# Last FFN, second pass: rounded gelu values read in place by TensorE as fp16 halves, with a smaller part of them sent out and back

## What is computed

```python
def _quant_per_tensor(x):
    scale = jnp.maximum(jnp.max(jnp.abs(x)), MIN_RANGE) / QP     # QP = 127
    return (_ste_round(x / scale), scale)

def _qlinear(x2d, w, b):
    xq, sx = _quant_per_tensor(x2d)
    wq, sw = _quant_per_tensor(w)
    out = jnp.matmul(xq, wq.T) + b[None, :]
    return out * (sw * sx)

h = _qlinear(x.reshape(-1, D), w1, b1)      # 256 -> 1024
h = jax.nn.gelu(h, approximate=False)
o = _qlinear(h, w2, b2)                     # 1024 -> 256
x = x + jnp.tanh(g_ffn[1]) * o
```

## Time and profile before

| | |
|---|---|
| runs | 1312.6, 1309.03, 1311.22 us; median 1311.22 |
| profiled execution | 1308.02 us, of which the span of the instructions 1306.2 |
| busy: TensorE, VectorE, ScalarE, GpSimd | 1192.7, 1119.0, 1012.5, 840.1 us |
| mean granted clock of TensorE | 0.979 |
| moved by DMA | 172.00 MB |

### The profile page before, as it was taken

The page is one execution under the profiler, slowest core; times in us unless marked ns, Lnnn a source line. Parts: engine busy times, 40 slices in busy tenths (PEclk is TensorE's granted clock), DMA queues, the critical chain, the costliest instruction groups (busy, mean ns, idle before and its releaser), DMA issues.

```text
span 1306.2 us, 30953 instructions
## 1 busy us (share of the span) xinstructions
PE 1192.7 (91%) x11668; PEld 852.7 (65%) x11668; DVE 1119.0 (86%) x1829; ACT 1012.5 (78%) x1737; POOL 840.1 (64%) x1315
## 2 busy tenths in 40 slices
PE   4699999999999999999998999998799888399898
PEld 3367777777777777777764666666678666144476
DVE  3488989899999998988879899988569899889898
ACT  2388888888887887888867999996456655799897
POOL 3157687777878678687776888776026777797000
PEclk9999999999999999999999999998999889699999
DMA  9677778779778687667410000001565363076199
GB/s 154 119 155 141 170 172 158 143 143 182 139 173 158 129 188 129 124 129 127 92 44 1 1 2 1 2 2 63 171 163 125 101 157 95 1 312 267 58 403 377
DMA packets 127939, 172.00 MB, mean 132 GB/s; under 512 B 47650, under 2 KB 79522, under 8 KB 123426
## 3 DMA queue, kind: packets, MB, share of 16 engines
q1 hardware_dynamic: 127024, 169.24, 54.3%
q10 hardware_dynamic: 768, 0.79, 0.5%
HBM read 80.79 MB, written 37.22 MB: 90 GB/s over the span
## 4 chain that ended last, share of the span: by engine, by line
PE 45%; POOL 16%; DVE 15%; ACT 13%; issue 6%; DMA 3%; SPq 2%; ACTq 0%; DVEq 0%; POOLq 0%
PE psum L615 7%; PE psum L630 6%; PE psum L597 4%; ACT f_gelu L2230 4%; PE psum L585 3%; POOL rs L935 3%; PE psum L1084 3%; PE psum L642 3%; PE psum L660 3%; ACT f_gelu L2222 3%; PE psum L1125 2%; POOL a_fac L1929 2%; PE psum L560 2%; PE psum L1619 2%; DVE f_hid L1245 2%
## 5 line engine op out<-in xcount | busy, mean ns | idle before, releaser
L743 ACT ACTIVATE exp_t<-psum 128x512 f32<-128x512 f32 x512 | 278.5, 599 | 98.5 <-PE psum L615 98.5
L815 DVE TENSOR_REDUCE neg_max<-psum 128x8 f32<-128x1024 f32 x256 | 312.6, 1221 | 31.0 <-PE psum L597 24.4
L935 POOL TENSOR_TENSOR rs<-rs,minus_half 128x16 f32<-128x16 f32 x64 | 187.2, 2925 | 5.0
L615 PEld LDWEIGHTS psum<-q_stack,k_stack 50*128 50x128 f32 x2048 | 133.4, 186 | 74.6 <-ACT exp_t L743 39.5
L615 PE MATMUL psum<-q_stack,k_stack 50*128 50x128 f32 x2048 | 169.7, 285 | 0.5 <-ACT exp_t L743 0.5
L630 PE MATMUL psum<-exp_t,v_pad 128*32 128x256 f32 x2048 | 137.0, 385 | 0.4 <-DVE x_state L846 0.4
L597 PE MATMUL psum<-k_stack,q_stack 48*128 48x256 f32 x1024 | 119.1, 310 | 19.7 <-DVE neg_max L815 17.2
L1084 PE MATMUL psum<-f_w,f_xqt 128*128 128x512 bf16 x512 | 122.4, 381 | 1.6 <-DVE f_hid L1245 1.1
L927 POOL TENSOR_TENSOR sq<-u 128x256 f32<-128x256 f32 x64 | 39.3, 615 | 117.0 <-DVE u L836 117.0
L106 DVE BATCH_NORM_STATS2 norm_stats<-x_state 128x6 f32<-128x256 f32 x256 | 101.9, 411 | 11.5 <-DMA x_state<-in_x 11.4
L1929 POOL TENSOR_TENSOR a_fac<-a_fac,a_expo 128x16 f32<-128x16 f32 x16 | 52.3, 3271 | 72.8 <-DVE a_fac L1835 72.4
(11 more groups left out here) (239 smaller groups left out, 3029.9 us busy)
## 6 DMA issues: line engine op xcount, KB each, us to landing
k_stack<-k_hi SPq DMA_DIRECT2D x252, 128.0 KB, 4.4
g_scratch<-f_gelu SPq DMA_DIRECT2D x18, 1024.0 KB, 4.7
k_stack<-k_lo SPq DMA_DIRECT2D x126, 128.0 KB, 4.5
f_gelu<-g_scratch SPq DMA_DIRECT2D x12, 1024.0 KB, 12.0
ctx_t<-in_ctx_t SPq DMA_DIRECT2D x32, 256.0 KB, 5.2
x_state<-in_x SPq DMA_DIRECT2D x16, 512.0 KB, 6.6
v_in<-in_ctx SPq DMA_DIRECT2D x32, 256.0 KB, 4.5
v_scratch<-v_in SPq DMA_DIRECT2D x32, 256.0 KB, 4.7
```

The costliest lines, as they stand in the source:

```text
L615: r = e.matmul(psum[:, bank + j, o:o + P], self.k_st[rows, b // 2 % self.NK, pair // 2 % 2, pair % 2, i, pair // 4, b % 2, :], self.q_st[r ...
L743: e.activation(self.prob[:, n % 3, j].rearrange("p n w t -> p (n w t)"), psum[:, self.score_bank(n) + j, :], ACT.Exp).then_inc(s["exp"], 1)
L815: e.tensor_reduce(self.negm[:, b % 2, :, :, 2 * u:2 * u + 2].rearrange("p j w n -> p j n w"), psum[:, 0:2, :].rearrange("p j (n w k) -> p ...
L935: e.tensor_tensor(self.rs[:, i], self.rs[:, i], self.expo[:, :], ALU.pow).then_inc(s["pool"], 1)
```

## The change

The numbers that stay on chip and how they reach TensorE are changed, in the second pass of Ffn1.

- The rounding constant is ROUND_HALF = ROUND + 0x6600. The low 16 bits of the fp32 sum, read as fp16 (`low_half`: every second 16-bit element, a step of 4 bytes), are then the rounded value plus HALF = 1536. TensorE takes them as its stationary operand where they lie; w2 is fp16. `round_off` and the buffer hq are gone.
- The 1536 too many in each of the 1024 products are taken back: `sums` makes the column sums of w2 once, on TensorE; VectorE splits them into a high and a low bf16 row (`split_sums`) and GpSimd puts the high one into place four times (`place_rows`); in each group, behind the seventh unit, four matmuls over 32 rows each (minus_half, sum_rows) subtract them. The four bias matmuls at a group's head are gone.
- 12 of the 64 units (`rounded_by_dve`) are rounded by VectorE, 52 by ScalarE.
- b2 is added to x by VectorE (`add_b2`, four for a group), after `scale_b2`, with no part in PSUM.
- The freed memory takes more units: a ring of 12 pairs, and 6 pairs behind it (three in xqt, two in `late`, one in parts of xqt and of the used weights w1). 18 pairs, 36 units, stay and 14 pairs go out and return. A pair is fetched into the place of pair FREED[r], once TensorE has used it.
- `keep_busy(8)` becomes `sums` and `keep_busy(4)`.

```diff
--- before.py
+++ after.py
@@ -2019,48 +2019,55 @@
-    H, NHT, CH, RING, EARLY = 1024, 8, 512, 22, 4
-    PLACED = 3
+    H, NHT, CH, RING, EARLY = 1024, 8, 512, 24, 4
+    PLACED = 6
...
-    ORDER = (list(range(NU // 2 - 4, NU // 2)) + list(range(NU // 2 - 8, NU // 2 - 4)) + list(range(NU // 2 - 12, NU // 2 - 8))
-             + [NOUT, NOUT + 1, NOUT - 2, NOUT - 1] + list(range(NOUT - 2)))
+    BEFORE_GATES = (143072 - 137536) // 4
+    ORDER = [4 * (7 - p) + i for p in range(4) for i in range(4)] + [NOUT, NOUT + 1, NOUT - 2, NOUT - 1] + list(range(NOUT - 2))
+    BACK = [NOUT - 2, NOUT - 1] + list(range(NOUT - 2))
+    FREED = [r for r in range(NOUT + 1) if r != 3]
     COUNTED = [1, 2, 3, 4, 5, 6, 7, 11]
-    BACK = [NOUT - 2, NOUT - 1] + list(range(NOUT - 2))
...
+    def rounded_by_dve(self, q):
+        return q % 8 == 1 or q % 16 == 12
...
-        self.hq = sb("f1_hq", [P, NHT, 2, CH], BF16)
+        self.late = sb("f1_late", [P, 2, 2, 2 * CH])
...
+    def unit(self, i, u):
+        if i < self.SLOTS + self.PLACED - 1:
+            return self.pair(i)[:, u].rearrange("p (j t) -> p j t", j=2)
+        if u:
+            return self.w16[0][:, :].bitcast(F32).rearrange("p (j t) -> p j t", j=2)
+        return self.xqt[:, :, :, :].rearrange("p h b t -> p h (b t)").bitcast(F32)[:, :, 6 * self.CH:7 * self.CH]
...
+    def wait_rounded(self, w, q):
+        on_dve = sum(self.rounded_by_dve(i) for i in range(q + 1))
+        w.wait_ge(self.s["hr_dve"], on_dve)
+        w.wait_ge(self.s["hr_act"], q + 1 - on_dve)
...
                 n = self.NOUT + r
-                w.wait_ge(s["hq"], 2 * r + 2)
+                q = 2 * self.FREED[r] + 1
+                w.wait_ge(s["o_pe"], 11 * (q // 8) + self.COUNTED[q % 8])
                 self.moved(w, n - self.NSEM)
...
+        def sums():
+            w.wait_ge(self.fw.s["w16"], 2)
+            w.wait_ge(s["sum_rows"], self.SUMMED)
+            w.wait_ge(s["gelu"], self.NU - 1)
+            for n in range(self.NHT):
+                r = e.matmul(psum[:, 5, 0:D], self.ones16, w2[:, n, :], start=n == 0, stop=n == self.NHT - 1)
+            r.then_inc(self.fw.s["pe"], 1)
         def project(p):
-            w.wait_ge(self.fw.s["w16"], 2)
-            w.wait_ge(s["b2"], 9)
             w.wait_ge(s["x_new"], 4 * (p - 1))
-            for i in range(4):
-                e.matmul(psum[:, 4 * (p % 2) + i, :], self.ones16[0:65, :], self.b2_rows[0:65, :], start=True, stop=False)
             for u in range(8):
                 q = 8 * p + u
                 n = 2 * (self.ORDER[q // 2] % 4) + q % 2
-                w.wait_ge(s["hq"], q + 1)
+                self.wait_rounded(w, q)
+                g = self.unit(self.slot(q // 2), q % 2)
                 for i in range(4):
                     for b in range(2):
                         t = 2 * i + b
-                        r = e.matmul(psum[:, 4 * (p % 2) + i, b * D:(b + 1) * D], self.hq[:, q % 8, t // 4, t % 4 * P:(t % 4 + 1) * P], w2[:, n, :],
-                                     start=False, stop=u == 7 and b == 1)
+                        r = e.matmul(psum[:, 4 * (p % 2) + i, b * D:(b + 1) * D], low_half(g[:, t // 4, t % 4 * P:(t % 4 + 1) * P]), w2[:, n, :],
+                                     start=u == 0 and b == 0, stop=u == 7 and b == 1)
                     if u == 7 or i == 3:
                         r.then_inc(s["o_pe"], 1)
+                if u == 6:
+                    w.wait_ge(s["sum_rows"], self.PLACED_ROWS)
+                    for i in range(4):
+                        rows = slice(32 * i, 32 * i + 32)
+                        e.matmul(psum[:, 4 * (p % 2) + i, :], self.minus_half[rows, :], self.sum_rows[rows, :].unsqueeze(1).to_broadcast([32, 2, D]),
+                                 start=False, stop=False)
...
-        keep_busy(8)
+        sums()
+        keep_busy(4)
...
-            e.activation(g, g, ACT.Copy, scale=self.m1[:, 5:6], bias=ROUND).then_inc(s["hr"], 1)
+            self.wait_back(w, q)
+            g = self.unit(self.slot(q // 2), q % 2)
+            e.activation(g, g, ACT.Copy, scale=self.m1[:, 5:6], bias=ROUND_HALF).then_inc(s["hr_act"], 1)
...
         for q in range(self.NU):
-            rounded(q)
+            if not self.rounded_by_dve(q):
+                rounded(q)
...
-        def round_off(q):
-            w.wait_ge(s["hr"], q + 1)
-            if q >= 8:
-                w.wait_ge(s["o_pe"], 11 * (q // 8 - 1) + self.COUNTED[q % 8])
-            e.tensor_scalar(self.hq[:, q % 8].rearrange("p j t -> p (j t)"),
-                            self.pair(self.slot(q // 2))[:, q % 2], ROUND, None, ALU.subtract).then_inc(s["hq"], 1)
+        def rounded(q):
+            self.wait_back(w, q)
+            g = self.unit(self.slot(q // 2), q % 2)
+            e.tensor_scalar(g, g, m1[:, 5:6], ROUND_HALF, ALU.mult, ALU.add).then_inc(s["hr_dve"], 1)
...
+        def add_b2(p, i):
...
+            e.tensor_tensor(sh.x[:, b:b + 2, :], sh.x[:, b:b + 2, :], self.b2[:, :].unsqueeze(1).to_broadcast([P, 2, D]), ALU.add).then_inc(s["prep"], 1)
...
+            w.wait_ge(s["prep"], self.B2_SCALED + 4 * p + i + 1)
...
-        w.wait_ge(s["prep"], self.G_OUT)
-        for q in range(self.NU + 8):
-            if q < self.NU:
-                round_off(q)
+        for q in range(-4, self.NU + 8):
+            if q == -4:
+                w.wait_ge(s["prep"], self.G_INV)
+            if q == -2:
+                split_sums()
+                scale_b2()
+            if q + 4 < self.NU and self.rounded_by_dve(q + 4):
+                rounded(q + 4)
             if q >= 8 and q % 8 in (1, 2, 3, 4):
                 add(q // 8 - 1, q % 8 - 1)
+            if 0 <= q < self.NU and q % 8 >= 4:
+                add_b2(q // 8, q % 8 - 4)
...
+        def place_rows():
+            for i in range(4):
+                w.wait_ge(s["sum_rows"], self.SPLIT + i)
                 row = slice(32 * i, 32 * i + 1)
...
+                e.tensor_copy(self.sum_rows[row, :], self.sum_high[row, :]).then_inc(s["sum_rows"], 1)
...
+        place_rows()
```

More of the change, by code:

```diff
@@ L2043, in __init__ @@
         CH, NHT = self.CH, self.NHT
[L2044 removed]
+        self.w16 = fw.w16 = [sb("f1_w16_" + n, [P, 2048], dt) for n, dt in (("up", BF16), ("down", F16))]
         self.b1 = sb("f1_b1", [P, NHT])
         self.b2 = sb("f1_b2", [P, D])
[L2047 to L2049 removed]
+        self.sum_high = sb("f1_sum_high", [P, D], BF16)
+        self.sum_rows = sb("f1_sum_rows", [P, D], BF16)
+        self.minus_half = sb("f1_minus_half", [P, P], BF16)
+        self.ones16 = self.sum_high[:, 0:P].bitcast(F16)
         self.xqt = sb("f1_xqt", [P, 2, NSEQ, P], BF16)
@@ L2077, in slot @@
         v = self.ORDER[r]
-        return self.own_slot(v) if v >= self.NOUT else self.slot(self.BACK.index(v))
+        return self.own_slot(v) if v >= self.NOUT else self.slot(self.FREED[self.BACK.index(v)])
     def own_slot(self, v):
@@ L2089, in pair, with wait_back @@
         halves = self.xqt[:, :, :, :].rearrange("p h b t -> p h (b t)").bitcast(F32)
+        if k >= 3:
+            return self.late[:, k - 3]
         return halves[:, :, 2 * n:3 * n] if k == 2 else halves[:, k, 0:2 * n].rearrange("p (u t) -> p u t", u=2)
+    def unit(self, i, u):
[4 more added lines that the diff above has]
+        return self.xqt[:, :, :, :].rearrange("p h b t -> p h (b t)").bitcast(F32)[:, :, 6 * self.CH:7 * self.CH]
+    def wait_back(self, w, q):
+        v = self.ORDER[q // 2]
+        if v < self.NOUT:
+            self.moved(w, self.NOUT + self.BACK.index(v))
+    def wait_rounded(self, w, q):
+        on_dve = sum(self.rounded_by_dve(i) for i in range(q + 1))
+        w.wait_ge(self.s["hr_dve"], on_dve)
+        w.wait_ge(self.s["hr_act"], q + 1 - on_dve)
     def moved(self, w, n):
@@ L2256, in find_max, with split_sums, scale_b2 @@
             w.wait_ge(s["gelu"], u + 1)
-            e.tensor_reduce(self.gmax[:, u:u + 1], self.pair(self.own_slot(u // 2))[:, u % 2], AX.X, ALU.max,
+            e.tensor_reduce(self.gmax[:, u:u + 1], self.unit(self.own_slot(u // 2), u % 2), AX.XY, ALU.max,
                             apply_absolute_value=True).then_inc(s["gmax"], 1)
-        def round_off(q):
-            w.wait_ge(s["hr"], q + 1)
-            if q >= 8:
-                w.wait_ge(s["o_pe"], 11 * (q // 8 - 1) + self.COUNTED[q % 8])
-            e.tensor_scalar(self.hq[:, q % 8].rearrange("p j t -> p (j t)"),
-                            self.pair(self.slot(q // 2))[:, q % 2], ROUND, None, ALU.subtract).then_inc(s["hq"], 1)
+        def rounded(q):
+            self.wait_back(w, q)
+            g = self.unit(self.slot(q // 2), q % 2)
+            e.tensor_scalar(g, g, m1[:, 5:6], ROUND_HALF, ALU.mult, ALU.add).then_inc(s["hr_dve"], 1)
+        def split_sums():
+            w.wait_ge(self.fw.s["pe"], self.fw.SPREAD + 5)
+            e.tensor_copy(self.sum_high[:, :], psum[:, 5, 0:D]).then_inc(s["sum_rows"], 1)
+            w.wait_ge(s["sum_rows"], self.SUMMED + 1)
```

(29 more changed lines are left out.)

19 lines of the change are left out of this document (8 added, 11 removed).

## The result

| | before | changed |
|---|---|---|
| median of the timed runs | 1310.12 us (4 runs) | 1301.16 us (4 runs, 1299.98 to 1302.69) |
| ratio, 95% interval | | 0.9932 (0.9916 to 0.9947) |
| profiled execution / its span | 1308.02 / 1306.2 | 1300.35 / 1298.5 |
| ScalarE's first rounding to the end of the span | 1306.2 - 1231.70 = 74.50 | 1298.5 - 1231.25 = 67.25 |

The last line of the table separates the second pass from everything before it, and will be used throughout: between the two profiled executions the pass itself became 7.25 us shorter, of which 6.8 had been forecast.

A forecast was written before the change was run, and what follows sets the result against it. ScalarE's roundings bound the second pass, TensorE next at 7.42 us a group. The last unit begins at 1292.9 instead of 1299.68, same tail: 6.8 us sooner, from the median 1311.22 to 1304.4 us; range 1301.5 to 1308.8.

The forecast's parts named there:

- ScalarE's pace as the old bound: Last FFN's second pass: ScalarE's roundings, 1.040 us each, set the old pace of 8.32 us a group.
- TensorE's need as the next bound: Second pass: TensorE needs 6.99 + 0.43 = 7.42 us a group, more than ScalarE's 6.76.
- Strided loads at nothing: TensorE's products: loading fp16 halves with a step of 4 bytes as stationary operand costs nothing extra.
- rival 2: Products' strided weight loads no longer hide: 1354 us if wholly exposed, 1317 if a quarter; chance 0.04.
- Rival 1: Corrections go one after the other: TensorE needs 7.85 us a group, kernel 1307.8 us; chance 0.10.
- VectorE and the order of its work: Second pass: VectorE needs 6.6 us a group and rounds a group ahead, holding up nothing TensorE needs.
- Transfers hidden: Second pass: 14 returned pairs, 23.1 MB moved, stay hidden with 2 us to spare for ScalarE, 10 for TensorE.
- The start: Head of second pass: sums and dense matmuls take 3.4 us as before; first product can start at 1234.38.
- Rival 4: Clock rises later at the pass's start: 7 us at 1.2 GHz cost 3.5 us, kernel 1307.9; chance 0.06.
- The tail "the same": Behind the last unit, the four adds and last output were taken to last as long as before.
- The chances: Forecast 0.74, rival 1 0.10, rival 2 0.04, rivals 3 and 4 0.06 each; faster 0.77, within 0.19, slower 0.04.
- rivals 3: Rival 3: returned pairs come late in the second pass if DMA falls to 330 GB/s; kernel 1306.5 us; chance 0.06.

The follow-up runs named there:

- early sums and three dense matmuls: Changed kernel with the column sums made before the exchange of the maximum and three dense matmuls after it: 1304.0 us, ratio to before 0.9949.
- the run with both: Changed kernel with early column sums, three dense matmuls after the exchange, and the last group's last three units done bank by bank: 1301.36 us.
- with four: Changed kernel with the column sums made before the exchange of the maximum and four dense matmuls after it: 1300.66 us.
- the run with bank order: Changed kernel with the last three units of the last group done one bank of sums after the other: 1301.05 us.

## Why the prediction was right in its steps and wrong in its number

- **ScalarE's pace as the old bound**: right. With all roundings back on it the distance is 8.32 again, and taking TensorE's bias matmuls away from the old pass changed nothing.
- **TensorE's need as the next bound**: right, 7.42 forecast, 7.42 measured. The two parts in it are 6.99 for the products and 0.43 for the corrections. The four hold TensorE for 0.33, and the step into them costs another 0.10 (64 products and that step take 7.09 between corrections): my allowance of 0.03 for changing between all rows and quarters was too small, that of 0.40 for the four by the same amount too large. That the two errors cancel to the exact 0.43 is luck. The Trainium skill ("TensorE: Matmul & The Clock Gate", section "Measured speedup vs the span model") with its 3.07 times comes near the four alone: an estimate by it is 0.96 / 3.07 = 0.31, against the 0.32 measured. The step from full-height products comes on top.
- **Strided loads at nothing**: right, and tested; rival 2 is gone. Rival 1 is gone too: the corrections don't go one after the other, and if they did they would cost 0.96, with the step 1.07, and not its 0.86.
- **VectorE and the order of its work**: right; 12.7 us idle before its adds, and TensorE waits for none of its roundings. Additions of b2 0.700, roundings 0.744 to 0.766, as taken.
- **Transfers hidden**: right for 14 pairs; with 18 the same pass is 9 us longer.
- **The start**: right to 0.03 us (first product 2.71 after ScalarE's first rounding, 2.68 forecast). Rival 4 didn't come true in the first profile of this kernel, where the clock was 1.00 from 1234 on; with early sums and three dense matmuls, and in the run with both, it did.
- **The tail "the same"**: too large by 0.47. From the last unit's start to the end it was 1306.2 - 1299.68 = 6.52 and is 1298.5 - 1292.45 = 6.05. Before, DMA was still behind with earlier outputs; now its share falls to 0.22 to 0.44 between 1292.5 and 1294.5 and the last output lands sooner. I had this as up to 0.6 in the range and nothing in the number. With it the sum is 7.25: 6.78 up to the last unit's start and 0.47 behind it.
- **What failed is the step from the sum to the time.** I put the sum against the median of three runs, 1311.22, and allowed 0.6 us for the runs' scatter at the lower end, though the three runs themselves lay 3.6 us apart. 29 later runs of before have their median at 1309.42 and reach from 1306.35 to 1314.12. So of the 3.2 us between number and result, 1.8 are the reference and 0.5 the tail. The remaining 0.9 no profile traces; it fits what the stages before the pass happened to take in four runs: the second measurement of the same kernel came out 0.5 slower, and 7.25 lies within the interval of its gain. Against 1309.42 the same sum gives 1302.6, and with scatter of 2 us in the range the result would have been inside. What makes the earlier stages differ by 3 us and more stays open.
- **The chances** don't add up as they were said: the forecast and halves of rivals 3 and 4 are 0.80 for faster, not 0.77, which leaves 0.16 for within.

## What to carry to other kernels

Where one engine paces a loop and another needs only a little less, work out the second one's need from a stretch in which it waited for nothing; moving work off the first is worth no more than the distance between the two, and each further cut on the second is then worth its full size. Price the transfers of a pass at the pace it will have, not the one it has: the bytes that were hidden at 8.3 us a group held up the pass at 7.4. When forecasting a time, the reference needs as much care as the sum: the median of three runs of a kernel whose earlier stages vary by 3 us can't be trusted to 0.6 us.

## What the runs showed of the hardware

- Four matmuls of 512 columns on four different quarters of the rows took 0.32 us, on one and the same quarter 0.96; changing from full-height products to quarters cost another 0.10 us a set (7.42 - 0.33 - 6.99).
- fp16 values with a step of 4 bytes, the low halves of fp32, load as stationary operand like packed ones: 98 ns, hidden beside a product every 0.109 us.
- After TensorE's rest of 1.65 to 2.5 us at the exchange of the maximum the granted clock took different courses in executions of nearly the same program. By stretches of 2 us from 1230 on: 0.59, 0.56, 1.00 in the changed kernel; 0.56, 0.50, 0.50, 0.73, 1.00 with early sums and three dense matmuls; 1.00 throughout with four. A rest of 0.24 (late rise) or 0.67 us (never lowered) before the first product didn't hold it down.
- Nearly all bytes of the last outputs had moved 2 us before the end in the run with bank order, at a DMA share of 0.14 and 0.02 from there on; the end waited for the last output to land.
